# The third token pool sorted one head group earlier, its expert tiles begun beside attention's last projections

## What is computed

```python
x = x + 0.5 * ffn(layernorm(x))
x = x + attn(layernorm(x))
x = x + 0.5 * ffn(layernorm(x))

# ffn: 16 experts of width 96, 2 per token
probs = softmax(x @ router_w)
w, idx = top_k(probs, 2);  w = w / sum(w)
h = silu(x @ gate_w[e]) * (x @ up_w[e])
out = sum over the two e of w_e * (h @ down_w[e])

# attn: 16 heads of 128, 4 key/value heads, rotary, causal
xqkv = x @ Wqkv
probs = softmax(scores / sqrt(128) + causal)
return attn @ Wo
```

## Time and profile before

| | us |
|---|---|
| median of 3 runs (917.87 to 919.81) | 918.38 |
| the profiled execution | 918.7 |
| its span | 916.9 |
| PE busy in it | 810.7 (88%) |
| DVE busy | 634.3 (69%) |
| ACT busy | 567.1 (62%) |
| POOL busy | 468.3 (51%) |
| first head group of batch 3 starts | 616.91 |
| last head group starts | 743.48 |
| first expert tile of the second mixture on PE | 789.44 |

### The profile page before, as it was taken

How to read it: one execution, slowest core, us unless ns; L and a number is a source line. 1 busy time by engine, 2 the same in 40 slices (tenths; PEclk the granted TensorE clock), 3 DMA queues, 4 the chain that set the end, 5 groups by cost and what they waited for, 6 DMA issues and landing times.

```text
span 916.9 us, 16344 instructions
## 1 busy us (share of the span) xinstructions
PE 810.7 (88%) x4904; PEld 687.1 (75%) x4904; DVE 634.3 (69%) x1503; ACT 567.1 (62%) x1458; POOL 468.3 (51%) x409
## 2 busy tenths in 40 slices
PE   4578989879999999998999999998999979799990
PEld 3567868668787888887888887787788767687870
DVE  6525565447887778878777878787766788455573
ACT  3245646557776777767777777676867646355550
POOL 1355413496775845755456555455454537203274
PEclk9999989999999999999999999999999999899995
DMA  9988963220011100000000000000000035456684
GB/s 340 324 277 297 267 170 116 83 39 13 12 15 16 19 1 7 12 7 1 1 1 2 1 2 1 1 3 1 8 1 1 1 149 168 123 151 196 195 241 169
DMA packets 55540, 78.60 MB, mean 86 GB/s; under 512 B 7840, under 2 KB 44320, under 8 KB 54816
## 3 DMA queue, kind: packets, MB, share of 16 engines
q1 hardware_dynamic: 43360, 55.50, 19.0%
q0 software_dynamic: 9216, 16.82, 7.4%
q10 hardware_dynamic: 2880, 5.24, 1.9%
HBM read 42.61 MB, written 34.93 MB: 85 GB/s over the span
## 4 chain that ended last, share of the span: by engine, by line
PE 55%; POOL 14%; issue 11%; DVE 7%; DMA 5%; SPq 4%; ACT 3%; POOLq 0%; ACTq 0%; DVEq 0%
PE ps L1492 46%; PE ps L1681 5%; SPq L705 3%; POOL sb_x L1430 3%; POOL xs L1405 2%; POOL xs L1412 2%; POOL sb_ropeB L1439 2%; POOL sb_xf L1442 2%; PE ps L1549 2%; DMA xs<-sb_wA_raw 1%; POOL sb_wF L1449 1%; DMA xs<-sb_wF_raw,sb_pos 1%; PE ps L1561 1%; DVE sb_nmax L1282 1%; DVE sb_x L1308 1%
## 5 line engine op out<-in xcount | busy, mean ns | idle before, releaser
L1492 PE MATMUL ps<-sb_wF 128*128 128x512 f32 (+3 forms) x1248 | 301.8, 368 | 7.5 <-DVE sb_wF L1299 4.4
L1492 PEld LDWEIGHTS ps<-sb_wF 128*128 128x128 f32 x1248 | 199.3, 192 | 23.3 <-DVE sb_wF L1288 3.3
L1439 POOL TENSOR_TENSOR sb_ropeB<-sb_ropeB,sb_sin 128x512 f32<-128x512 f32 x80 | 107.0, 1337 | 151.9 <-ACT sb_ropeB L885 151.8
L902 ACT ACTIVATE sb_prob<-ps,sb_nmax 128x128 f32<-128x128 f32 (+3 forms) x256 | 134.2, 526 | 62.8 <-DVE sb_nmax L1282 61.7
L1492 PE MATMUL ps<-sb_wF,sb_wA 128*128 128x512 f32 x576 | 156.8, 408 | 7.4 <-ACT sb_ropeB L885 7.1
L1282 DVE TENSOR_REDUCE sb_nmax<-ps 128x1 f32<-128x128 f32 (+3 forms) x256 | 121.9, 485 | 59.1 <-PE ps L1492 57.6
L1449 POOL TENSOR_TENSOR sb_wF<-sb_xf,sb_wF 128x512 fp32r<-128x512 f32 x75 | 98.6, 1315 | 95.3 <-ACT sb_wF L894 95.0
L1308 DVE SCALAR_TENSOR_TENSOR sb_x<-ps,sb_rinv,sb_x 128x256 f32<-128x256 f32 x256 | 122.8, 480 | 23.3 <-PE ps L1492 14.4
L1288 DVE TENSOR_TENSOR sb_wF<-ps,sb_wF 128x512 fp32r<-128x512 f32 x160 | 109.4, 684 | 28.3 <-ACT sb_wF L910 27.6
L1492 PE MATMUL ps<-sb_wA,sb_wF 128*128 128x256 f32 x768 | 115.7, 287 | 10.3 <-DVE sb_x L1308 8.6
L1492 PEld LDWEIGHTS ps<-sb_wF,sb_wA 128*128 128x128 f32 x576 | 103.7, 192 | 27.4 <-ACT sb_ropeB L885 8.2
(11 more groups left out here) (175 smaller groups left out, 1233.1 us busy)
## 6 DMA issues: line engine op xcount, KB each, us to landing
ys<-sb_wA_raw SPq DMA_DIRECT2D x124, 128.0 KB, 2.5
sb_wF_raw<-xs SPq DMA_DIRECT2D x44, 128.5 KB, 3.7
sb_wA_raw<-xs SPq DMA_DIRECT2D x44, 128.5 KB, 2.6
xs<-sb_wA_raw SPq DMA_DIRECT2D x19, 256.0 KB, 12.4
sb_work<-xs SPq DMA_DIRECT2D x36, 128.5 KB, 3.4
...
sb_wF_raw<-in_wgu SPq DMA_DIRECT2D x4, 768.0 KB, 15.7
...
```

Of the source, the lines that this page charges most:

```text
L902: nc.scalar.activation(prob[k % 2][:, h, 0:(i + 1) * P], ps[:, bank_of((k * G + h) % (UB * G)), 0:(i + 1) * P], ACT.Exp, bias=nmax[:, k % ...
L1439: nc.gpsimd.tensor_tensor(ropeB[:, slot], ropeB[:, slot], sin[:], ALU.mult).then_inc(rope_mul, 1)
L1492: return nc.tensor.matmul(out, lhsT, rhs, start=start, stop=stop)
```

## The change

Five things, all in one diff.

1. Pool 2 is sorted earlier. Batches 0 and 1 get their norms in groups 1.3 and 2.3 (`early_norm`, results in the new tile `early`), batch 2 at the end of 3.0. Rows are normalised in 3.0 and 3.1. Pairs stand in 3.0 (three) and 3.1 (three) instead of 3.1 (four) and 3.2 (two). Routing, ranks, shares and places are in 3.2. The scatters stay first in group 3.3's list on POOL.
2. W,3,0 and W,3,1 leave `ORDER_LAST` and stand inside the first step of `experts(1)`; W,3,1 writes to `OBANK`. PE's wait for all additions goes, a wait for W,3,0's stands before the first down product, and DVE waits for all of them before its first weighted copy.
3. SP loads the first ten tiles before it waits for the last transposes and fetches pool 3's tables.
4. The weights come from tanh of half the gap: w = 0.25 ± 0.25 tanh, in place of exp, addition and reciprocal.
5. In the second mixture the gathers go token tile by token tile (both experts in turn), and batch 3 is stored in four parts.

```diff
@@ lists of the last group
-        T,3,2 V,3,0 V,3,1 W,2,0 T,3,3 V,3,2 W,2,1 V,3,3 W,3,0 W,3,1""",
+        T,3,2 V,3,0 V,3,1 W,2,0 T,3,3 V,3,2 W,2,1 V,3,3""",
...
@@ turn_of
-            if b < B - 1 and g == 1 and engine == "pool":
-                items = items + [("power", 0, 3 + b)]
-            if b == B - 2 and g == KV and engine == "pool":
-                items = spread(items, [("power", 0, B + 2)], 0.35, 0.4)
+            if g == 1 and engine == "pool":
+                items = items + [("power", 0, (3, 4, 6)[b])]
+            if g == 3 and b > 0 and engine == "pool":
+                items = spread(items, [("power", 0, (5, 7)[b - 1])], 0.65, 0.7)
+            if g == 3 and b > 0 and engine == "dve":
+                items = spread(spread(items, [("early", b - 1, n) for n in range(4)], 0.05, 0.55),
+                               [("early", b - 1, n) for n in (4, 5)], 0.85, 0.9)
...
@@ SHARES
-        "act": {0: [(0.6, 0.8, range(7))], 1: [(0.0, 0.05, range(7, 8)), (0.7, 0.8, range(12, 16))]},
+        "act": {0: [(0.05, 0.5, range(7))], 1: [(0.0, 0.05, range(7, 8)), (0.2, 0.4, range(12, 16))]},
...
-LOGIT_AFTER = [(1, -1, 3), (1, 0, 0), (1, 1, 0), (1, 1, 1), (2, -1, 3), (2, 0, 0)]
+LOGIT_AFTER = [(0, 0, 0), (0, 1, 0), (0, 1, 1), (1, 0, 0), (1, 1, 0), (1, 1, 1), (2, 1, 0)]
...
@@ SP
-        sp.wait_ge(pt_done, B * PB)
-        router_constants(pools[3])
-        rank_constants(pools[3])
-        tiles(pools[2], pools[3])
+        def last_constants():
+            sp.wait_ge(pt_done, B * PB)
+            router_constants(pools[3])
+            rank_constants(pools[3])
+
+        tiles(pools[2], pools[3], last_constants)
...
+        for t in range(T):
+            sp.wait_ge(gadd_done, 2 * T * (B - 1) + 2 * (t + 1))
+            sp.dma_start(A["out"][B - 1][:, t], x[:, B - 1, t]).then_inc(out_done, 16)
...
@@ ACT
-            nc.scalar.activation(gap(q, 1), gap(q, 0), ACT.Exp).then_inc(gexp_done, 1)
+            nc.scalar.activation(gap(q, 1), gap(q, 0), ACT.Tanh, scale=-0.5).then_inc(gtanh_done, 1)
...
@@ DVE shares
-            link(nc.vector.tensor_scalar(y, e, 1.0, None, ALU.add))
-            link(nc.vector.reciprocal(y, y))
-            step(nc.vector.tensor_scalar(row_weights(q), y, 0.5, None, ALU.mult))
-            nc.vector.scalar_tensor_tensor(wgt[:, q.t0:q.t0 + q.nt], e, 0.5, y, ALU.mult, ALU.mult)\
+            step(nc.vector.tensor_scalar(row_weights(q), tanh, 0.25, 0.25, ALU.mult, ALU.add))
+            nc.vector.tensor_scalar(wgt[:, q.t0:q.t0 + q.nt], tanh, -0.25, 0.25, ALU.mult, ALU.add)\
...
@@ DVE experts
+                if q.p == 2 and i == 0:
+                    x_add(B - 1, UB - 1, 0)
+                    x_add(B - 1, UB - 1, 1)
                 if has_tile(n, at):
                     h(at)
+                if q.p == 2 and i == 0:
+                    x_add(B - 1, UB - 1, 2)
+                    x_add(B - 1, UB - 1, 3)
+                    dve.wait_ge(xadd_done, G * UB * B)
...
@@ PE
+            if s == pools[2].tiles:
+                pe.wait_ge(xadd_done, G * UB * B - G // 2)
...
+            elif q.p == 2 and i == 0:
+                project(B - 1, UB - 1, 0)
+                project(B - 1, UB - 1, 1)
...
-        pe.wait_ge(xadd_done, G * UB * B)
         pe.wait_ge(w_in[1], W_LANDED)
         experts(1)
```

More of the change, by code:

```diff
@@ L131, in program @@
     rs = sb("rs", [P, 4, T], F32)
+    early = sb("early", [P, 2, (B - 2) * T], F32)
     with ExitStack() as own:
@@ L652, in load_at, with pair @@
         return u if odd == 0 and 0 <= u < LATE else None
-    def pair(j):
+    def pair(n, j):
+        if n == 1:
+            return divmod(j, 2)
         b, r = divmod(j, 2 * T)
@@ L718, in store_tile, with tiles @@
             sp.dma_start(ys[q.p][s * P:(s + 1) * P, :], yo(at)).then_inc(y_out[at % RING], 16)
-        def tiles(first, second):
+        def tiles(first, second, then=lambda: None):
             loads = [(first, s) for s in range(first.ns)] + [(second, s) for s in range(second.ns)]
@@ L955, in _ @@
                 normalise(pools[1], j)
-        gap_exp(pools[1])
+        gap_tanh(pools[1])
         experts(0)
@@ L1244, in third @@
                 rsqrt_start(m, s)
-            elif n2 == 2:
+            elif n == 4:
                 rsqrt_step(s)
-            else:
-                rsqrt_end(m, s)
+            elif n == 5:
+                rsqrt_end(m, s)
+            elif n < 12:
+                lcopy(q, n - 6)
+            elif n < 19:
+                route(q, n - 12)
+            elif n == 19:
+                places(q, 0)
+                places(q, 1)
+            elif n == 20:
+                shares(q)
+                places(q, 2)
+            else:
+                places(q, 3)
@@ new lines, in early_norm @@
+        def early_norm(b, n):
+            if n < 2:
+                if n == 0:
+                    dve.wait_ge(xadd_done, G * UB * (b + 1))
+                norm_stats(stats, b, 2 * n, 2 * n)
+                norm_stats(stats, b, 2 * n + 1, 2 * n + 1)
+            elif n == 2:
+                mean_start(stats, mv)
+            elif n == 3:
+                rsqrt_start(mv, rs)
+            elif n == 4:
+                rsqrt_step(rs)
+            else:
+                own = slice(b * T, (b + 1) * T)
+                nc.vector.scalar_tensor_tensor(early[:, 0, own], mv[:, 0], -1.0, rs[:, 1], ALU.mult, ALU.mult)
+                nc.vector.tensor_copy(early[:, 1, own], rs[:, 1]).then_inc(ln_done, 1)
@@ L1328, in do @@
                     weights_low(n)
+                elif what == "early":
+                    early_norm(k, n)
                 elif n < 2:
@@ L1492, in mm @@
             return nc.tensor.matmul(out, lhsT, rhs, start=start, stop=stop)
-        projections = {"act": 0, "dve": 0, "logits": 0}
-        def projection_bank():
-            pe.wait_ge(proj_act, projections["act"])
-            pe.wait_ge(proj_dve, projections["dve"])
+        third = {"logits": 0, "ranks": 0}
         def logit_transposes(q, h):
@@ L1527, in logits @@
             if q.p == 2:
-                projections["logits"] = copies(q, h)
+                third["logits"] = copies(q, h)
         def ranks(q):
@@ L1534, in ranks @@
             if q.p == 2:
-                projection_bank()
+                pe.wait_ge(pt_lo, third_tile(RANKS))
+                third["ranks"] = q.p + 1
             R = ranks_at(q)
@@ L1675, in prob_transposes @@
                 pe.wait_ge(pt_lo, b * PB + tb - 1)
-            if projections["logits"]:
-                pe.wait_ge(lcopy_done, projections["logits"])
+            if third["logits"]:
+                pe.wait_ge(lcopy_done, third["logits"])
+            if third["ranks"]:
+                pe.wait_ge(rank_read, third["ranks"])
             for h in range(G):
@@ L1702, in project @@
             pe.wait_ge(a_lo, b * UB + k + 1)
-            if not (b == 0 and k == 0 and half == 0):
+            if wo_bank(b, k, half) == WBANK and not (b == 0 and k == 0 and half == 0):
                 pe.wait_ge(xadd_done, G * (b * UB + k) + 2 * half)
```

102 lines of the change are left out of this document (50 added, 52 removed), and 12 rows, old and new, of the table AFTER.

## The result

The changed kernel takes 909.71 us in the median of 4 runs (908.59 to 910.09), the kernel before 919.1 in the 4 runs beside them; the ratio is 0.9897 (95% interval 0.9881 to 0.9912), 9.4 us faster. The forecast was 903.7, 14.7 faster, in a range of 899.5 to 910.5. The direction and the range hold; the sum is 5.3 us too large, and 909.71 lies outside the forecast's own range of 900.5 to 906.5.

The account below looks back on a forecast made before the run. The prediction took PE's work as the bound, with excess from the third pool's work and waits, the seam and a table load. Its terms summed to -14.7 us off the 918.38 median, giving 903.7, range 899.5 to 910.5.

Parts of the forecast that it names:

- A: Norms of batches 0 and 1 moved into groups 1.3 and 2.3: +0.4 us, between 0 and +6.
- B: Group 3.0, statistics leaving its head and three pairs of router transposes and logits coming in: -0.4 us, between -1.2 and +2.
- C: Group 3.1, four pairs of router transposes and logits becoming three: -3.0 us, between -3.9 and -1.
- D: Group 3.2, two pairs leaving, ranks, shares and places coming in, routing earlier: -1.0 us, between -2.5 and +1.3.
- E: Group 3.3 and seam: first tile 8.8 us earlier, then halves +1.8, additions +0.5, clock -1.2; sum -7.7, between -9.3 and -4.5.
- F: Tanh for exp, removing both ACT table loads beside the last pool: -2.5 us, between -2.0 and -2.6.
- G: Last stores, the final one shrinking from 512 to 128 KB: -0.5 us, between 0 and -1.
- tiles late: Rival at the seam: scatters land slowly under the weights' transfer, PE idles at low clock; 906.9 us, chance 0.20.
- DVE becomes the bound, one for one: Rival: added DVE work in groups 1.3, 2.3 and 3.2 lengthens them equally; -7.1 us, 911.3 us, chance 0.09.
- knock-on rival: Each us DVE gets in groups 1.3, 2.3 and 3.2 costs r us; at r = 2 +2.7, 921.1 us; chance 0.05.

Follow-up runs that it names:

- e3: Changed kernel with the five DVE instructions of batch 2's mean in group 3.0 moved later, away from POOL's rotary step; 910.41 us, ratio 0.9901.
- e11: Changed kernel with five scatters in flight, batch 2's mean and batches 0 and 1's roots moved, three routing parts moved to group 3.1's end; 902.09 us, ratio 0.9808.
- e4: Changed kernel with the reading of the ranks in group 3.2 placed ahead of two maxima and a copy of the probabilities; 909.55 us, ratio 0.9897.
- e8: Changed kernel with scatters, mean, roots and three routing parts re-placed, projection halves ahead of the tiles; 965.03 us on a disturbed chip, not comparable whole.
- e2: Changed kernel with five instead of three first scatters of the third pool in flight before POOL waits for a landing; 907.85 us, ratio 0.9869.
- e10: Changed kernel with the last two projection halves and their four DVE additions back ahead of the expert tiles; 905.76 us, ratio 0.9855.

## Why the prediction was right, and where its sum was off

| term | forecast | measured | from |
|---|---|---|---|
| A norms in 1.3, 2.3 | +0.4 | +1.5 | 35.59 - 34.67, 35.59 - 35.01 |
| B group 3.0 | -0.4 | +2.45 | 43.04 - 40.59 |
| C group 3.1 | -3.0 | -3.6 | 39.73 - 43.35 |
| D group 3.2 | -1.0 | -0.1 | 42.52 - 42.63 |
| E to the first tile | -8.8 | -7.7 | 38.30 - 45.96 |
| E behind it | +1.1 | +1.7 | 17th down product: 817.23 - 780.81 - (824.13 - 789.44) |
| F | -2.5 | -2.4 | 17th to 19th down product: 3.00 - 5.42 |
| G | -0.5 | -0.2 | 5.46 - 5.65 |

From first to last tile the changed kernel takes 98.26 us and the kernel before 98.96 (789.44 to 888.40), 0.7 less, which is +1.7 - 2.4. The measured terms sum to -8.3; the rest of the 10.1 us of the profiled executions is an earlier start of the first head group (-1.7, the spread of the runs), +0.5 in the other groups and -0.6 from the last tile to the last addition.

**B** is the step that failed most, by 2.9 us. I costed three pairs of transposes and logits at 1.45 us of PE and a wait of 0.8. The price of a pair was right ((40.44 - 36.14)/3 = 1.43; in 3.1 it was 1.46), but I put the pairs on PE's 35.01 us of group 2.3, and group 3.0 had 36.14 before, without any pair: 1.1 us. The rest is waits, 2.6 us instead of 0.8, and 2.17 of them are the one for the copy. I had looked for what DVE adds in instructions and took 0.2 us each; that two of them would stand beside POOL's rotary step and take 1.25 us was not in the sum. e3 shows it: placed elsewhere, the wait is gone, and PE is busy 40.45 of 40.89 us.

**A** failed in the same way, by 1.1 us: I took the cover as given because DVE idles 7.6 us in the group. It does, but the root's first instruction was caught by POOL (1.23 us), and the copy behind it reached PE 0.8 us late. In e11 the term is gone (34.59 in both groups). The trace of the kernel before had a case of it at just this instruction, the root of batches 0 and 1 in group 3.0:

```profile
635.34 1.24 DVE L1002 TENSOR_TENSOR sb_frsC<-sb_frsC 128x8 f32<-128x8 f32 x1 [1.63 <-POOL sb_frsC L1387]
...
635.28 1.28 POOL L1449 TENSOR_TENSOR sb_wF<-sb_xf,sb_wF 128x512 fp32r<-128x512 f32 x1
```

The prediction weighed that mechanism at D and set it aside, since the routing steps stood beside POOL already. "SBUF — State Buffer" of the Trainium skill (section "Who interferes with whom") says that a DVE instruction with both inputs in SBUF contends with a GpSimd instruction that reads SBUF. The traces agree: 1.25 and 1.23 us beside POOL, 0.15 and 0.16 away from it. The error was to apply the rule to the large routing steps alone and not to the small statistics that the change moves.

**C** was right but for 0.6: PE was busy 39.39 us as forecast, and the waits were 0.3, not 0.9.

**D** was 0.9 too hopeful, and in the waits. The group had 3.1 us without PE before (42.63 - 39.53) and I added 1.5. In e3, where the clock stays up in it, PE is busy 36.19 of 42.28 us, so 6.1 are idle; 1.88 of them are the wait for the ranks (1.92 in the changed kernel), named beforehand as what would show it wrong, and 2.27 one for a rotary product. e4 shows that the place of that one reading was not the cause. e11 and e8 show that DVE's load has a part in it: three parts less in 3.2 gave 0.8 us there with the clock down in both kernels (42.52, 41.76) and 1.9 with it up (42.28, 40.35), for 0.8 in 3.1. A rival stands untested: about 1.1 us of the reading is POOL's stretch of L1123, in e4 that of L1127 and in e11 still one of 1.14 us, and no run puts the reading where POOL idles.

**E.** The mechanism was right: scatters start before the group, and the waits at its start go. The first tile was 1.2 us later than forecast, 38.3 us after the group's start and not 37.1 (780.6 - 743.48). The delay by the first landing was priced about right: 2.1 us are in the forecast (780.6 - 778.5), and the wait was 2.29, which e2 takes off. What came late was the first scatter, 0.5 us ahead of the group's start and not 1.4. So "tiles late" is true in its mechanism, though not in its size: PE idled 3.04 us, over the 2 us named beforehand as a sign of error, and the clock fell, yet up to the first tile 7.7 of the 8.8 us came. Behind the first tile the halves cost 2.1 us (forecast 2.3), and it is the clock that gave back less than 1.2. At the fourth down product the kernel before stands at 11.76 us and e10, with the clock up and the halves ahead too, at 9.58, so the low clock had cost 2.2; the changed kernel still pays 1.8. Its wait at the seam was 3.04 us, and the forecast's condition, that PE stays busy, did not hold.

That "DVE becomes the bound, one for one" got A wrong (+1.5, not +6) and D too dear (+1.0 against -0.1). The knock-on rival did not come: by its formula A gives r = 0.25 (6r = 1.5) and D r = 0.7 (3.8r - 2.8 = -0.1). The result lies nearer to the total of "one for one" (911.3) than to the forecast, though the cause was not that one. A, B, D and E missed in the same direction, and 0.8 us more would have left the range (910.5), so that it held is in part luck.
